# Loading the stacked attention operands in three transfers of 48, 32 and 16 rows

## The chip, the cores and the metric

The kernel runs on one core of one Trainium2 chip. The metric is the device time of one execution in microseconds (us), lower is better. The median of three runs of the kernel before is 3266.39 us (3259.58 to 3267.85).

## The reference

The computation is one block: half a mixture-of-experts feed-forward step, relative-position attention, half a feed-forward step again. The change touches attention alone, whose core is:

```
q, k, v = (w @ Wq.T), (w @ Wk.T), (w @ Wv.T)      # split in 16 heads of 16 values
rp = (r @ Wr.T)                                   # r: 2*Lq-1 sinusoidal positions
AC = einsum('bhid,bhjd->bhij', q + u_bias, k)
BD = einsum('bhid,hjd->bhij', q + v_bias, rp)
BD = _rel_shift(BD)
attn = softmax((AC + BD) * scale)
out = einsum('bhij,bhjd->bhid', attn, v)
```

There are 2 batches of 2048 tokens, so 32 heads in all, each with a score matrix of 2048 x 2048.

## The kernel before

The program has three stages: feed-forward and projections (to about 370 us), attention (to about 3140 us), the last feed-forward.

Each float32 operand of AC and BD is split in three bfloat16 parts that add up to it (`qu_parts`, `qv_parts`, `k_parts`, `pos_parts`, all in DRAM, part number first, then head and value, then position). A product of two float32 numbers becomes six products of parts. So each operand is stacked in SBUF as six blocks of 16 rows, 96 rows (`STACK`), and one matmul over 96 rows sums all six. The query side takes parts `Q_PARTS = (0, 0, 0, 1, 1, 2)`, the key and position side `K_PARTS = (0, 1, 2, 0, 1, 0)`. Rows 0 to 47 thus hold query part 0 three times against key parts 0, 1, 2, rows 48 to 79 query part 1 twice against key parts 0, 1, and rows 80 to 95 query part 2 against key part 0. A row of `qu`, `qv` or `ks` has 2048 values (4 KB), one of `pos` 4096 values (8 KB). All are double buffered. `qu`, `qv` and `ks` are loaded for every head, `pos` for every pair of heads (the same head of the two batches).

Attention goes by tiles of 128 queries, 16 to a head (`NI`), 512 in all. Each engine has a `body(step, k)` for tile k. 192 tiles are written out and run twice in a loop, between 4 tiles ahead and 124 behind. In `body(k)` TensorE (PE) transposes the scores of tile k (line 837), weighs values with it and the tile before (L851), makes position scores for tile k + 15 (L771) and content scores for tile k + 2 (L823). ScalarE (ACT) copies position scores to the buffer `score` (L895, L897) and takes the exponential (L905). VectorE (DVE) adds content and position scores for tile k + 2 (L958) and copies the transposes (L967).

The relative shift is done by DMA. For each group of four tiles GpSimd (POOL) waits for ACT's last copy of the group, and then issues 31 moves `score<-score` (L663) from SBUF to SBUF. Each has an access with two partitions outermost. DVE's first addition of a group waits for them (`moved`); it stands in the body of every fourth tile, with k = 2 modulo 4.

SyncE (SP) issues all loads (`load_head` at L682, `load_pos` at L696, `load_vs` at L701, `store` at L706). Its body names a tile for each block (`QV_BLOCK_AT`, `POS_BLOCK_AT`, `KS_BLOCK_AT`, `VS_AT`), but it has no wait of its own in most tiles. What holds it is `positions_made` before the first block of `qv` (tile 5 of a head) and of `pos` (tile 4 of a pair), `contents_made` before the first block of `ks` (tile 13), the wait for `weighed` before `vs` (tile 9), and the wait for `fin_used` before the store (tile 3). Between these it issues one after another, as fast as it can.

Of the kernel before, what the change touches and what calls it, by code (L numbers as in the profile page):

```python
# [28 lines left out]
Q_PARTS = (0, 0, 0, 1, 1, 2)  # L29
K_PARTS = (0, 1, 2, 0, 1, 0)  # L30
# [3 lines left out]
def build_program(nc, x, wq_t, wk_t, wv_t, wr_t, u_bias, v_bias, w_in, w_out, pos_t, ident, fold, iota, out):  # L34
# [22 lines left out]
    with ctx:  # L57
# [464 lines left out]
        with ExitStack() as c2:  # L522
# [53 lines left out]
            block = c2.enter_context(nc.Block())  # L576
            NLOAD = 16 * len(Q_PARTS)

# [17 lines left out]
            def head_there(step, h):  # L596
                return there(step, h, NT // NI, HEADS)
# [77 lines left out]
            def _(sp):  # L675
                def head(step, h):

                    return h % NB * H + step * (NT // PAIR) + h // NB

                def load_head(dst, src, order, step, h, loaded, blocks):  # L680
                    for i in blocks:
                        sp.dma_start(dst[h % 2][i * DH:(i + 1) * DH, 0:L],  # L682
                                     src[order[i], bass.ds(head(step, h) * DH, DH), :]).then_inc(loaded[h % 2], 16)

                def load_qu(step, h, blocks):
                    load_head(qu, qu_parts, Q_PARTS, step, h, qu_loaded, blocks)

                def load_qv(step, h, blocks):
                    load_head(qv, qv_parts, Q_PARTS, step, h, qv_loaded, blocks)
# [29 lines left out]
                def body(step, k):  # L719
                    h = k // NI + 2  # L720
                    if k % NI in QV_BLOCK_AT and head_there(step, h):
                        if k % NI == QV_BLOCK_AT[0]:
                            positions_made(step, k + POS_AHEAD)
                        load_qv(step, h, [QV_BLOCK_AT.index(k % NI)])
                    pair = k // PAIR + 1
                    if k % PAIR in POS_BLOCK_AT and there(step, pair * PAIR):
                        if k % PAIR == POS_BLOCK_AT[0]:
                            positions_made(step, k + POS_AHEAD)
                        load_pos(step, pair, [POS_BLOCK_AT.index(k % PAIR)])
                    at = (k + NI - KS_FIRST) % NI  # L730
                    h = (k + NI - KS_FIRST) // NI + 1
                    if at in KS_BLOCK_AT and h > 1 and head_there(step, h):
                        if at == 0:
                            contents_made(step, k + AC_AHEAD)
                        load_ks(step, h, [KS_BLOCK_AT.index(at)])
                        load_qu(step, h, [KS_BLOCK_AT.index(at)])
                    h = k // NI + 1
# [7 lines left out]
                for u in range(2):  # L745
                    sp.sem_inc(output_stored[u], 16)
                every = range(len(Q_PARTS))
                load_pos(0, 0, every)
# [368 lines left out]
```

## Time and profile before

| | |
|---|---|
| median of three runs | 3266.39 us |
| profiled execution, its own time | 3262.82 us |
| span of its instructions | 3261.0 us |
| of it attention, first to last transpose | about 2698 us |
| PE, DVE, ACT, POOL busy | 90, 81, 77, 71% |
| data moved by DMA | 657.31 MB, mean 202 GB/s |

The profiled execution stands 3.6 us under the median. "PE busy" includes matmuls that overlap; "idle" in the rows is the engine's time before an instruction, and the name behind an arrow is what ended it. SPq stands for SP's sequencer, and its times are those of issuing a transfer. "Us to landing" runs from issue to the last of a transfer's completions. The share of a DMA queue is the time of its packets, as a share of 16 engines over the span.

### The profile page before, as it was taken

How to read it: one execution, taken by the hardware profiler on the slowest of the kernel's cores; microseconds unless marked ns; L12 is line 12 of the kernel's file. 1: busy time of each engine (PE TensorE's matmuls, PEld its weight loads, DVE VectorE, ACT ScalarE, POOL GpSimd, SP SyncE). 2: the span in 40 equal slices, each digit the busy share in tenths (PEclk: the TensorE clock that was granted, in tenths of full speed). 3: DMA queues.
4: the chain of work that ended last, by engine and by line, in shares of the span. 5: the costliest groups of instructions: out<-in, count | busy, mean ns of one | idle time of the engine just before them, and what ended most of it. 6: DMA issues, size and time to landing. Idle time of an engine off the chain costs nothing. (4 is left out here: it accounts for less than half of the span.)

```text
span 3261.0 us, 110511 instructions
## 1 busy us (share of the span) xinstructions
PE 2923.0 (90%) x40768; PEld 2056.2 (63%) x40768; DVE 2636.0 (81%) x5042; ACT 2501.7 (77%) x3850; POOL 2317.9 (71%) x4135
## 2 busy tenths in 40 slices
PE   4556479999999999998999999999999999999955
PEld 1444146767676767676767666767767676767635
DVE  2555158989898989897989888989989898989976
ACT  2333468989888888887988888888888898889832
POOL 3333487878788878787878888787878787878810
PEclk8777679999999999999999999999999999999977
DMA  6333688888888888887888988888888888888841
GB/s 198 97 110 97 145 205 216 224 217 224 220 221 225 222 217 221 218 221 194 222 219 222 229 216 221 222 218 220 223 221 221 212 225 216 223 224 224 213 128 52
DMA packets 290221, 657.31 MB, mean 202 GB/s; under 512 B 189472, under 2 KB 256928, under 8 KB 272288
## 3 DMA queue, kind: packets, MB, share of 16 engines
q0 software_dynamic: 190960, 526.89, 61.6%
q1 hardware_dynamic: 98736, 123.38, 13.5%
q8 instruction: 335, 5.49, 0.7%
q14 instruction: 190, 1.56, 0.2%
HBM read 77.19 MB, written 46.14 MB: 38 GB/s over the span
## 5 line engine op out<-in xcount | busy, mean ns | idle before, releaser
L663 POOL DMA_DIRECT2D score<-score x3999 | 2186.3, 550 | 560.8 <-ACT score L897 491.4
L895 ACT COPY score<-pos_bank 128x512 f32<-128x512 f32 x2048 | 1105.4, 597 | 330.6 <-PE pos_bank L771 329.0
L905 ACT ACTIVATE score<-score,low 128x1024 f32<-128x1024 f32 x1024 | 1196.9, 1170 | 34.5 <-DVE low L958 30.3
L967 DVE COPY prob_t<-pt_bank 128x512 f32<-128x512 f32 x1792 | 1162.0, 684 | 5.3 <-PE pt_bank L837 2.9
L837 PE MATMUL pt_bank<-ident_sb,score 128*128 128x128 f32 x8192 | 1092.7, 276 | 12.8 <-ACT score L905 6.1
L837 PEld LDWEIGHTS pt_bank<-ident_sb,score 128*128 128x128 f32 x8192 | 958.3, 143 | 225.4 <-issue 52.3
L958 DVE CUSTOM_DVE_ANT_0 score<-ac_bank,score 128x1024 f32<-128x1024 f32 x512 | 627.1, 1225 | 295.5 <-DMA score<-score 153.2
L771 PE MATMUL pos_bank<-pos,qv 96*32 96x512 bf16 (+14 forms) x12160 | 666.5, 318 | 61.9 <-DMA qv<-qv_parts 43.1
L958 DVE CUSTOM_DVE_ANT_0 score<-ac_bank,score,low 128x1024 f32<-128x1024 f32 x512 | 657.2, 1284 | 66.1 <-PE ac_bank L823 58.4
L851 PE MATMUL acc_bank<-prob_t,vs 128*32 128x128 f32 x16384 | 667.0, 280 | 5.6 <-issue 5.5
L823 PE MATMUL ac_bank<-ks,qu 96*128 96x512 bf16 x2048 | 626.5, 388 | 44.8 <-DVE low L958 44.4
L851 PEld LDWEIGHTS acc_bank<-prob_t,vs 128*32 128x32 f32 x16384 | 388.2, 109 | 181.5 <-issue 180.0
L771 PEld LDWEIGHTS pos_bank<-pos,qv 96*32 96x32 bf16 x12160 | 324.9, 98 | 133.2 <-issue 63.0
L823 PEld LDWEIGHTS ac_bank<-ks,qu 96*128 96x128 bf16 x2048 | 116.4, 97 | 363.1 <-DVE low L958 241.7
L509 POOL CAST part<-rest 128x512 bf16<-128x512 f32 x64 | 50.7, 792 | 224.6 <-DVE rest L462 224.6
L913 ACT COPY prob_t<-pt_bank 128x512 f32<-128x512 f32 x256 | 150.0, 586 | 41.8 <-PE pt_bank L837 41.7
L809 PEld LDWEIGHTS pos_bank<-fold_sb,acc_sb 128*128 128x128 f32 x1024 | 135.3, 193 | 21.1 <-issue 2.0
L809 PE MATMUL pos_bank<-fold_sb,acc_sb 128*128 128x32 f32 x1024 | 126.4, 267 | 2.1 <-issue 1.4
L239 PE MATMUL bank_one<-ident_sb,normed_one 128*128 128x128 f32 x128 | 30.2, 426 | 93.4 <-DVE normed_one L148 93.4
L920 ACT COPY acc_sb<-acc_bank 128x512 f32<-128x512 f32 x128 | 75.0, 586 | 30.7 <-PE acc_bank L851 26.0
L462 DVE SCALAR_TENSOR_TENSOR rest<-proj,bias_sb,part 128x512 f32<-128x512 f32 x32 | 36.7, 1212 | 71.7 <-ACT part L443 71.7
L239 PEld LDWEIGHTS bank_one<-ident_sb,normed_one 128*128 128x128 f32 x128 | 25.8, 226 | 98.2 <-DVE normed_one L148 98.2
(95 smaller groups left out, 989.8 us busy)
## 6 DMA issues: line engine op xcount, KB each, us to landing
score<-score POOLq DMA_DIRECT2D x3937, 129.5 KB, 5.4
pos<-pos_parts SPq DMA_DIRECT2D x96, 128.0 KB, 9.7
qv<-qv_parts SPq DMA_DIRECT2D x192, 64.0 KB, 7.2
ks<-k_parts SPq DMA_DIRECT2D x192, 64.0 KB, 7.6
qu<-qu_parts SPq DMA_DIRECT2D x192, 64.0 KB, 7.1
v_heads<-v_sb SPq DMA_DIRECT2D x8, 1024.0 KB, 7.3
vs<-v_heads SPq DMA_DIRECT2D x32, 256.0 KB, 6.9
pos_parts<-part SPq DMA_DIRECT2D x16, 384.0 KB, 3.0
```

The costliest lines, as they stand in the source:

```text
L663: pool.dma_start(shifted(odd, s, groups, 0), shifted(odd, s, groups, QUAD - 1 - s))\
L771: last = pe.matmul(dst[row:row + QUAD, col + lo:col + hi], lhsT=qv[k // NI % 2][:, q0:q0 + QUAD], rhs=pos[u][:, at + lo:at + hi], start=Tr ...
L809: last = pe.matmul(POS[FOLD_AT % 3][:, f * VW:(f + 1) * VW], lhsT=acc_sb[:, f * P:(f + 1) * P], rhs=fold_sb[:, :], start=True, stop=True)
L823: last = pe.matmul(AC[:, c * BANK:(c + 1) * BANK], lhsT=qu[u][:, i * P:(i + 1) * P], rhs=ks[u][:, first:first + BANK], start=True, stop=True)
L837: last = pe.matmul(PT[c % 2][:, t * P:(t + 1) * P], lhsT=score[:, slot(k), c * BANK + t * P:c * BANK + (t + 1) * P], rhs=ident_sb[:, :], i ...
L851: last = pe.matmul(ACC[t * VW:(t + 1) * VW, f * P:(f + 1) * P], lhsT=vs[k // NI % 2][:, 4 * c + t, :], rhs=prob_t[:, c, t * P:(t + 1) * P] ...
L895: act.copy(score[:, at + f, c * BANK:(c + 1) * BANK], ring(m)[:, :]).then_inc(pos_out, 1)
L905: act.activation(cols, cols, ACT.Exp, bias=low[:, slot(k), NH - 1:NH], scale=-1.0)\
L913: act.copy(prob_t[:, c, :], PT[c % 2][:, :]).then_inc(copied_act, 1)
L920: act.copy(acc_sb[:, :], ACC[:, :]).then_inc(acc_out, 1)
L958: dve.tensor_tensor_reduce(cols, AC[:, :], cols, SCALE, low[:, slot(k), h - 1:h] if h else -NEG, ALU.add, ALU.min, low[:, slot(k), h:h + 1 ...
L967: dve.tensor_copy(prob_t[:, c, :], PT[c % 2][:, :]).then_inc(copied, 1)
```

## The change

Each operand is loaded in three transfers (`RUNS = ((0, 3), (3, 2), (5, 1))`: first block and count) of 48, 32 and 16 rows, in place of six of 16 rows. For queries the source is one part, repeated by a zero step in front: its access is 3 (step 0) x 16 x 2048, and 2 x 16 x 2048. For keys and positions it is `k_parts[0:3, 16 rows, :]`, 3 x 16 x 2048 (or x 4096), and 2 x 16. The destination is 48 or 32 partitions. The bytes are the same.

The tiles named for the loads change: `qv` from 5 to 11 of a head to 8, 10, 12; `ks` from 13 to 19 to 13, 15, 17; `qu`, so far beside `ks`, to 19, 21, 23; `pos` from 4 to 11 of a pair to 18, 22, 32; `vs` from 9 to 14.

```diff
-            NLOAD = 16 * len(Q_PARTS)
+            RUNS = ((0, 3), (3, 2), (5, 1))
+            NLOAD = 16 * len(RUNS)
...
-                def load_head(dst, src, order, step, h, loaded, blocks):
+                def rows_of_run(i):
+
+                    return slice(RUNS[i][0] * DH, (RUNS[i][0] + RUNS[i][1]) * DH)
+
+                def load_queries(dst, src, step, h, loaded, blocks):
                     for i in blocks:
-                        sp.dma_start(dst[h % 2][i * DH:(i + 1) * DH, 0:L],
-                                     src[order[i], bass.ds(head(step, h) * DH, DH), :]).then_inc(loaded[h % 2], 16)
+                        part = src[i, bass.ds(head(step, h) * DH, DH), :].rearrange("(o d) n -> o d n", o=1)
+                        sp.dma_start(dst[h % 2][rows_of_run(i), 0:L], part.to_broadcast([RUNS[i][1], DH, L]))\
+                            .then_inc(loaded[h % 2], 16)
...
                 def load_ks(step, h, blocks):
-                    load_head(ks, k_parts, K_PARTS, step, h, ks_loaded, blocks)
+                    for i in blocks:
+                        sp.dma_start(ks[h % 2][rows_of_run(i), :],
+                                     k_parts[0:RUNS[i][1], bass.ds(head(step, h) * DH, DH), :])\
+                            .then_inc(ks_loaded[h % 2], 16)
 
                 def load_pos(step, pair, blocks):
                     for i in blocks:
-                        sp.dma_start(pos[pair % 2][i * DH:(i + 1) * DH, :],
-                                     pos_parts[K_PARTS[i], bass.ds((step * (NT // PAIR) + pair) * DH, DH), :])\
+                        sp.dma_start(pos[pair % 2][rows_of_run(i), :],
+                                     pos_parts[0:RUNS[i][1], bass.ds((step * (NT // PAIR) + pair) * DH, DH), :])\
                             .then_inc(pos_loaded[pair % 2], 16)
...
-                POS_BLOCK_AT = (4, 6, 7, 8, 10, 11)
-                KS_FIRST, KS_BLOCK_AT, QV_BLOCK_AT, VS_AT = 13, (0, 1, 2, 3, 5, 6), (5, 6, 7, 8, 10, 11), 9
+                POS_FIRST, POS_BLOCK_AT = PAIR // 2 + 2, (0, 4, 14)
+                KS_FIRST, KS_BLOCK_AT, QU_BLOCK_AT = 13, (0, 2, 4), (6, 8, 10)
+                QV_BLOCK_AT, VS_AT = (8, 10, 12), 14
...
-                for load in (load_qv, load_ks, load_qu):
+                for load in (load_qv, load_ks):
                     load(0, 1, every)
+                load_qu(0, 1, [i for i in every if QU_BLOCK_AT[i] < FIRST + NI - KS_FIRST])
+                load_pos(0, 1, [i for i in every if POS_BLOCK_AT[i] < PAIR - POS_FIRST])
```

Only SP's instructions change; those of PE, ACT, DVE and POOL stand as they did. Two places on SP, from the pair of heads that begins at tile 32. "ISA" rows are register work and waits; sizes are those of the destination, partitions first.

SP before, in the first half of a pair, from tile 4 on:

```order
L696 ISA [waits pos_full]
L696 DMA pos0<-pos_parts 16x4096
L128 ISA
L682 ISA [waits pos_full]
L682 DMA qv0<-qv_parts 16x2048 x2
L696 ISA
L696 DMA pos0<-pos_parts 16x4096
L682 DMA qv0<-qv_parts 16x2048
```

SP now, from tile 8 on:

```order
L688 ISA [waits pos_full]
L688 DMA qv0<-qv_parts 48x1x2048
L688 ISA
L688 DMA qv0<-qv_parts 32x1x2048
L688 ISA
L688 DMA qv0<-qv_parts 16x2048
```

The blocks of `pos` have gone from here, and `qv` comes three tiles later, in three transfers behind one wait.

SP before, from tile 13 of a pair on, `ks` beside `qu`, six of each, and then the store:

```order
L682 DMA ks0<-k_parts 16x2048 [waits ac_full]
L682 DMA qu0<-qu_parts 16x2048
L682 DMA ks0<-k_parts 16x2048
...
L706 ISA [waits fin_used]
L706 DMA attended<-head_out 128x256
```

SP now, from tile 18 of a pair on:

```order
L705 ISA [waits pos_full]
L705 DMA pos1<-pos_parts 48x1x4096
L688 DMA qu0<-qu_parts 48x1x2048
L128 REGISTER_ALU
L715 ISA [waits fin_used]
L715 DMA attended<-head_out 128x256
L688 DMA qu0<-qu_parts 32x1x2048
L705 DMA pos1<-pos_parts 32x1x4096
L688 DMA qu0<-qu_parts 16x2048
```

Five loads and the store now follow one wait for `pos_full`: the wait for `fin_used` behind it is for work of the same tile.

## Rows read from the trace of the kernel before

**Rows 1.** The page, part 1: busy us, share of the span, instructions.

```profile
PE 2923.0 (90%) x40768; PEld 2056.2 (63%) x40768; DVE 2636.0 (81%) x5042; ACT 2501.7 (77%) x3850; POOL 2317.9 (71%) x4135
```

**Rows 2.** Windows of one head each: heads 13 and 21 (odd), 14 and 20 (even).

```profile
core 0: us, PE busy (x) PEld busy (x) DVE busy (x) ACT busy (x) POOL busy (x), PEclk, DMA share, GB/s
1553.78:1635.24 81.46, 81.46 (x1245) 58.49 (x1244) 74.97 (x129) 73.56 (x114) 67.50 (x124) 1.00 0.83 224
1635.25:1723.17 87.92, 83.93 (x1245) 58.97 (x1244) 74.96 (x129) 73.96 (x114) 67.79 (x125) 0.98 0.84 217
...
2142.70:2230.61 87.91, 84.33 (x1245) 59.45 (x1244) 74.97 (x129) 73.97 (x114) 67.81 (x125) 0.98 0.85 217
2230.62:2312.31 81.69, 81.53 (x1245) 58.51 (x1244) 75.01 (x129) 73.56 (x114) 68.03 (x126) 1.00 0.83 225
```

**Rows 3.** Windows of four tiles each in head 14: tiles 4 to 7, 8 to 11.

```profile
1657.57:1677.94 20.37, 20.37 (x312) 14.69 (x311) 18.76 (x33) 18.38 (x30) 13.88 (x26) 1.00 0.72 187
1677.95:1702.81 24.86, 22.14 (x312) 15.28 (x311) 18.72 (x33) 18.57 (x30) 20.78 (x39) 0.93 1.04 260
```

**Rows 4.** Waits of DVE from 500 to 3100 us: us in total, times, longest.

```profile
DVE score L958 <- PE ac_bank L823: 184.2, 337, 4.2
DVE score L958 <- DMA score<-score: 86.9, 37, 6.6
```

**Rows 5.** Timeline in head 14, DVE, then PE: start, duration, instruction, idle time before.

```profile
1691.79 1.23 DVE L958 CUSTOM_DVE_ANT_0 score<-ac_bank,score 128x1024 f32<-128x1024 f32 x1 [4.22 <-DMA score<-score]
...
1691.84 0.87 PE L837 MATMUL pt_bank<-ident_sb,score 128*128 128x128 f32 x5 [2.72 <-issue]
1692.64 1.08 PE L851 MATMUL acc_bank<-prob_t,vs 128*32 128x128 f32 x16
```

**Rows 6.** Timeline of SP's issues in head 14.

```profile
1667.26 2.46 SPq L682 DMA_DIRECT2D qv<-qv_parts  x2
1669.91 1.80 SPq L696 DMA_DIRECT2D pos<-pos_parts  x1
...
1677.05 1.85 SPq L696 DMA_DIRECT2D pos<-pos_parts  x1
1684.79 0.35 SPq L701 DMA_DIRECT2D vs<-v_heads  x1
```

**Rows 7.** Timeline of POOL's issues in head 14: one group's moves, the next begin.

```profile
1667.02 14.76 POOL L663 DMA_DIRECT2D score<-score  x27 [1.10 <-issue]
1684.09 16.40 POOL L663 DMA_DIRECT2D score<-score  x30 [2.31 <-ACT score L897]
```

**Rows 8.** DMA queues from 500 to 3100 us: packets, MB, share of 16 engines.

```profile
q0 software_dynamic: 183083, 506.17, 74.2%
q1 hardware_dynamic: 28633, 58.21, 8.6%
```

**Rows 9.** DMA issues of the whole run: transfers, KB each, median us to landing.

```profile
score<-score POOLq DMA_DIRECT2D x3937, 129.5 KB, 5.4
pos<-pos_parts SPq DMA_DIRECT2D x96, 128.0 KB, 9.7
qv<-qv_parts SPq DMA_DIRECT2D x192, 64.0 KB, 7.2
...
vs<-v_heads SPq DMA_DIRECT2D x32, 256.0 KB, 6.9
...
qu_parts<-part SPq DMA_DIRECT2D x16, 384.0 KB, 2.9
...
score<-score POOLq DMA_DIRECT2D x62, 64.8 KB, 2.8
```

**Rows 10.** Timeline at the start of attention: SP's first issues, PE's first matmuls.

```profile
372.68 2.68 SPq L696 DMA_DIRECT2D pos<-pos_parts  x6
375.41 2.73 SPq L682 DMA_DIRECT2D qv<-qv_parts  x6
...
383.88 1.94 PE L771 MATMUL pos_bank<-pos,qv 96*32 96x32 bf16 x20 [43.08 <-DMA qv<-qv_parts]
```

More of the change, by code:

```diff
@@ L678, in head @@
                     return h % NB * H + step * (NT // PAIR) + h // NB
-                def load_head(dst, src, order, step, h, loaded, blocks):
+                def rows_of_run(i):
+                    return slice(RUNS[i][0] * DH, (RUNS[i][0] + RUNS[i][1]) * DH)
+                def load_queries(dst, src, step, h, loaded, blocks):
                     for i in blocks:
-                        sp.dma_start(dst[h % 2][i * DH:(i + 1) * DH, 0:L],
-                                     src[order[i], bass.ds(head(step, h) * DH, DH), :]).then_inc(loaded[h % 2], 16)
+                        part = src[i, bass.ds(head(step, h) * DH, DH), :].rearrange("(o d) n -> o d n", o=1)
+                        sp.dma_start(dst[h % 2][rows_of_run(i), 0:L], part.to_broadcast([RUNS[i][1], DH, L]))\
+                            .then_inc(loaded[h % 2], 16)
                 def load_qu(step, h, blocks):
-                    load_head(qu, qu_parts, Q_PARTS, step, h, qu_loaded, blocks)
+                    load_queries(qu, qu_parts, step, h, qu_loaded, blocks)
                 def load_qv(step, h, blocks):
-                    load_head(qv, qv_parts, Q_PARTS, step, h, qv_loaded, blocks)
+                    load_queries(qv, qv_parts, step, h, qv_loaded, blocks)
                 def load_ks(step, h, blocks):
-                    load_head(ks, k_parts, K_PARTS, step, h, ks_loaded, blocks)
+                    for i in blocks:
+                        sp.dma_start(ks[h % 2][rows_of_run(i), :],
+                                     k_parts[0:RUNS[i][1], bass.ds(head(step, h) * DH, DH), :])\
+                            .then_inc(ks_loaded[h % 2], 16)
                 def load_pos(step, pair, blocks):
                     for i in blocks:
-                        sp.dma_start(pos[pair % 2][i * DH:(i + 1) * DH, :],
-                                     pos_parts[K_PARTS[i], bass.ds((step * (NT // PAIR) + pair) * DH, DH), :])\
+                        sp.dma_start(pos[pair % 2][rows_of_run(i), :],
+                                     pos_parts[0:RUNS[i][1], bass.ds((step * (NT // PAIR) + pair) * DH, DH), :])\
                             .then_inc(pos_loaded[pair % 2], 16)
@@ L724, in body @@
                         load_qv(step, h, [QV_BLOCK_AT.index(k % NI)])
-                    pair = k // PAIR + 1
-                    if k % PAIR in POS_BLOCK_AT and there(step, pair * PAIR):
-                        if k % PAIR == POS_BLOCK_AT[0]:
+                    at = (k + PAIR - POS_FIRST) % PAIR
+                    pair = (k + PAIR - POS_FIRST) // PAIR + 1
+                    if at in POS_BLOCK_AT and there(step, pair * PAIR):
+                        if at == 0:
                             positions_made(step, k + POS_AHEAD)
-                        load_pos(step, pair, [POS_BLOCK_AT.index(k % PAIR)])
+                        load_pos(step, pair, [POS_BLOCK_AT.index(at)])
                     at = (k + NI - KS_FIRST) % NI
@@ L735, in body @@
                         load_ks(step, h, [KS_BLOCK_AT.index(at)])
-                        load_qu(step, h, [KS_BLOCK_AT.index(at)])
+                    if at in QU_BLOCK_AT and (h > 1 or k >= FIRST) and head_there(step, h):
+                        load_qu(step, h, [QU_BLOCK_AT.index(at)])
                     h = k // NI + 1
@@ L746, in _ @@
                     sp.sem_inc(output_stored[u], 16)
-                every = range(len(Q_PARTS))
+                every = range(len(RUNS))
                 load_pos(0, 0, every)
```

## The prediction

> **What bounds the kernel now.** I read the page's busy shares first, then windows of one head each, and then the waits and the timeline where a head is slow. PE is busy 90% of the span, more than any other engine [rows 1], and in a quiet head it is busy all the time: head 13 takes 81.46 us with 81.46 us of PE, and head 21 81.69 us with 81.53 [rows 2]. That is the floor, 32 heads of it. It is not reached in even heads: heads 14 and 20 take 87.9 us for the same work [rows 2]. The four tiles 4 to 7 of head 14 still take 20.37 us, at a DMA share of 0.72; tiles 8 to 11 take 24.86 us, at a share of 1.04 (it can pass 1 by what is counted at a window's edge), and there PE is busy 22.14 us only, at a granted clock of 0.93 [rows 3]. The reader should see that PE does the same 312 matmuls and that the DMA engines are full. The timeline names the link: DVE waited 4.22 us for the moves `score<-score`, PE then stood for 2.72 us, and the 16 matmuls of L851 behind the stop took 1.08 us [rows 5]. Over the steady stretch DVE lost 86.9 us in 37 such waits; its larger sum for `ac_bank` is PE's own pace [rows 4].
>
> How thin the cover is follows from two rows. POOL's issues for that group ended at 1667.02 + 14.76 = 1681.78 us [rows 7]. DVE wanted the data at 1691.79 - 4.22 = 1687.57 us [rows 5]. So moves may land 5.8 us after the last issue; their median is 5.4 [rows 9]. Whatever adds more than half a microsecond to the landing of the last moves is paid in full. (A group's cover is about 1.1 us longer where POOL has not had the extra stop of 1.10 us that stands in rows 7.)
>
> **What the change removes.** The loads of `pos` leave the stretch in which `qv` and `vs` are loaded, and `qv` comes three tiles later. SP issued `qv` and `pos` in turn behind one wait, 1.2 us each or more, from 1667.26 to about 1679 us, inside the time in which the group's moves are issued and land [rows 6, 7]. With `pos` gone the share there falls back to that of an odd head. Odd heads show the result: 6.2 us less than the even ones in rows 2. Other even heads lose less, and the 86.9 us of rows 4 hold all such waits. I take 4.4 us for each of 16 even heads, 70 us. The bounds are 50 and 87 us. SP's issues fall from six to three for each operand; SP is waited for by nobody in the steady stretch, so I cost that at nothing.
>
> **What it adds: the same bytes on fewer DMA engines.** The question on which the sum turns is how many of the 16 DMA engines a transfer of 48 rows uses. The trace shows no such load, but it shows what an access with a small outermost count does. A move has two partitions outermost. With one stretch in each it carries 64.8 KB and lands after 2.8 us, with two stretches 129.5 KB after 5.4 us, while 384 KB with 128 partitions outermost land after 2.9 us [rows 9]. A transfer that was spread over 16 engines would not take 2.6 us longer for 65 KB. So two rows run on about two engines. The new sources have 3 or 2 outermost (with step 0 for queries), whatever the destination has. I take it that the 48-row transfers run on three engines and the 32-row ones on two, and that these are always the same, since no rotation shows for SP; that last point is an assumption.
>
> The Trainium skill (DMA: Bandwidth & Descriptors, "Why a DMA increments its semaphore by 16 and not by 1") says that the count of engines is the largest number up to 16 that divides both accesses' slowest dimension, and that a load from SP uses the lowest-numbered ones; by it the counts are 3 and 2, and the sum is the one below. No run here has shown it for loads from SP.
>
> The price. Queue q1 moved 58.21 MB in 8.6% of 16 engines' 2600 us, 3578 us of engine time, and q0 506.17 MB in 74.2%, 30867 us [rows 8]: 61 us a MB for both. A 48-row load of 196.6 KB gives each of three engines 65.5 KB, 4.0 us; a 32-row load gives each of two the same, 4.0 us; 16 rows on 16 engines give 4 KB, 0.25 us. `pos` has double rows, 8.0, 8.0 and 0.5 us. The two engines that are in both counts get, for each head, 3 x 8.25 us for `qv`, `ks` and `qu` and half of 16.5 for `pos`, 33 us. Before, each engine had 3 x 6 x 0.25 + 3 x 0.5 = 6 us. That is 27 us more for each head. The engines stand idle 16% of a head (shares of 0.83 to 0.85 [rows 2]), 13 us. So 14 us a head find no room: 450 us over 32 heads is the upper bound. The lower is 0: the 61 us a MB were measured with all 16 engines in each other's way, and 14 engines now lose some of their load, so the two may run faster and swallow all.
>
> Between these I go by the clumps, since that is what rows 5 show to be paid. In each pair of heads there are five places where one or two 4.0 us shares fall on the two engines while moves are in flight (`qv` at tiles 8 and 24, `ks` at 13 and 29, `qu` at 31, which nothing holds back), and one at tile 18 with 8 + 4 + 4 + 8 = 24 us behind a single wait. A move issued to these engines waits at least for the share ahead of it. With half a microsecond of cover, and some 2 us that the engines are idle between two groups' moves, I put 1 us on each of the five and 7 us on the 24 us clump, since moves and loads take turns and two groups share it. That is 12 us a pair, 190 us for 16 pairs. It is nearer to the lower bound than to the upper, because rows 3 show what an overfull stretch costs: tiles 8 to 11 of head 14 ran at a share of 1.04 and lost 4.5 us, not more.
>
> The first loads are on the path too. PE's first matmul waits for `pos` and `qv`, from the first issue at 372.68 us to 383.88 us [rows 10]. Now the two engines have 16.5 + 8.25 = 25 us of work before `qv` is whole, at the rate above, and at least half of it on an idle chip. The start comes 3 to 15 us later; I take 10. The loads of the next head and `pos` pair are queued right behind and meet the first moves: 3 us.
>
> The sum, against the profiled execution's own 3262.8 us: -70 + 190 + 13 = +133, 3396 us. The median of the runs stands 3.6 us higher, within their spread; I say **3395 us**.
>
> **Rivals.**
>
> *Sixteen engines after all (chance 0.20).* If 48 rows are spread by the destination, three rows to an engine, the bytes of each engine stay as they were and the collision goes: -70 us. Against that stands the clump of tile 18: 384 + 192 + 128 + 128 + 256 + 64 KB, 1.18 MB, 4.5 us on each engine, of which some 2 us were there before (`ks` and `qu`). 2.5 us more, less the 1.1 us of looser cover, is 1.4 us for each of 16 pairs, 22 us, and 10 us for `qv` closer to a landing. 3225 us: **faster**. For it: the destination's outermost count is a multiple of 16. Against it: the moves of rows 9. It decides at one point: whether source or destination sets the spread.
>
> *Few engines, but the moves slip through (0.12).* If an engine takes one packet of a load and one of a move in turn, 4 KB (0.25 us) ahead of each 2 us of a move delay the moves by an eighth only, and the loads bear the wait, which have over ten tiles to land. Then 50 us take the place of the 190: 3255 us, from no change to slightly faster. Against it: `vs` has 8 rows of 2 KB for each engine and `qv` one of 4 KB, and both land after about 7 us [rows 9]; eight turns behind moves would be longer by 14 us.
>
> The Trainium skill (DMA: Bandwidth & Descriptors, "Queues, rings and completion order") has each engine drain some 9 to 17 descriptors of one ring before it turns to another. By it a share of 16 rows passes in one or two turns, and the forecast holds; by turns of one it would be this rival. Rows 9 agree with the first in `vs`.
>
> *Two engines full (0.08).* If the 14 us a head are all paid: 3263 - 70 + 450 + 13, about 3655 us.
>
> **How the numbers follow.** The forecast has 0.60, with a range of its own from 3290 to 3540 us: its stalls can be 80 or 340 us. Of a difference under 0.3%, some 10 us, a measurement can't tell much from no change. The first rival is faster in 0.17 of its 0.20, the second in 0.05 with 0.04 within 0.3%, the forecast's low end gives 0.02 faster and 0.03 the same: faster 0.24, same 0.09, slower 0.67. The range for 8 in 10 leaves out the lower half of the first rival and the last one: 3220 to 3560 us.
>
> **What the profile will show.** If I am right, the 48-row and 32-row loads take 10 us and more to land while a 16-row one stays near 7; DVE's wait for the moves rises from 86.9 us to over 200; odd heads are slow as well as even ones, with the worst four tiles from 20 to 27 of a pair; the granted clock falls below 0.99; and the mean DMA share falls, since the span grows and the bytes don't. PE's start comes at 387 us or later. If the loads land after 7 or 8 us at every size and tiles 8 to 11 of even heads take 20.4 us, it was the first rival. If large loads land late and the wait for the moves is small, it was the second. What would break the sum without touching the mechanism is the clump of tile 18, its largest and least certain term.

## The result and the profile after

The changed kernel takes 3558.58 us, the median of 4 runs (3550.05 to 3564.23), beside 3265.6 us for the kernel before, the median of 4 (3259.58 to 3267.85). The ratio is 1.0883, interval 1.0859 to 1.0906: slower by 293 us where 129 was forecast. The profiled execution took 3550.05 us, 287.2 more than the profiled one before.

First part 1 of the page of after, then its DMA queue of SP's transfers (packets, MB, share of 16 engines), then windows of one head each: head 14 (even), head 15 (odd).

```profile
PE 2975.7 (84%) x40768; PEld 2083.4 (59%) x40768; DVE 2633.7 (74%) x5042; ACT 2504.0 (71%) x3850; POOL 2309.9 (65%) x4135
...
q1 hardware_dynamic: 90336, 123.35, 12.0%
```

```profile
core 0: us, PE busy (x) PEld busy (x) DVE busy (x) ACT busy (x) POOL busy (x), PEclk, DMA share, GB/s
1776.07:1871.83 95.76, 84.56 (x1245) 59.86 (x1244) 74.96 (x129) 73.69 (x114) 67.55 (x125) 0.93 0.74 196
1871.84:1960.98 89.14, 84.40 (x1245) 59.52 (x1244) 74.92 (x129) 73.69 (x114) 67.35 (x124) 0.96 0.78 209
```

No engine's busy time rose by more than 3 us but PE's, whose 2923.0 us [rows 1] became 2975.7 for the same instructions. Its granted clock in these heads is 0.93 and 0.96, where even and odd ones had 0.98 and 1.00 [rows 2]: a part of the time is spent at 1.2 GHz rather than 2.4, behind stops such as the one shown below (0.80 in its four tiles). Both kinds of head are slow now. The DMA share, 0.83 to 0.85 before, fell to 0.74 and 0.78, with the same bytes: the DMA engines taken together have more room than before, and data comes later all the same.

Next, the waits of DVE in after from 500 to 3400 us (total, times, longest).

```profile
DVE score L972 <- DMA score<-score: 358.4, 61, 14.5
DVE score L972 <- PE ac_bank L837: 180.3, 284, 2.7
```

The wait for the moves rose by 271 us, from 86.9 in 37 waits to 358.4 in 61 [rows 4]; the wait for PE stayed. Most of the loss sits in one place. Here are two windows of four tiles in after, tiles 0 to 3 of an even head (16) and of an odd one (17), and then the timeline around tile 2 of head 16: SP's issues, POOL's, DVE and PE.

```profile
1960.99:1994.72 33.73, 23.35 (x312) 16.03 (x311) 18.72 (x33) 18.56 (x30) 20.88 (x39) 0.80 0.78 208
2055.84:2077.31 21.47, 21.05 (x312) 14.41 (x311) 18.72 (x33) 18.57 (x30) 19.41 (x37) 1.00 0.87 234
```

```profile
1948.34 0.75 SPq L699 DMA_DIRECT2D ks<-k_parts  x1
1953.17 0.36 SPq L710 DMA_DIRECT2D vs<-v_heads  x1
1953.62 0.67 SPq L699 DMA_DIRECT2D ks<-k_parts  x1
1954.40 0.72 SPq L705 DMA_DIRECT2D pos<-pos_parts  x1
1955.22 1.51 SPq L699 DMA_DIRECT2D ks<-k_parts  x1
1956.82 0.75 SPq L688 DMA_DIRECT2D qu<-qu_parts  x1
```

```profile
1950.80 14.18 POOL L664 DMA_DIRECT2D score<-score  x26 [0.18 <-issue]
1967.13 16.89 POOL L664 DMA_DIRECT2D score<-score  x31 [2.16 <-ACT score L911]
```

```profile
1983.03 1.23 DVE L972 CUSTOM_DVE_ANT_0 score<-ac_bank,score 128x1024 f32<-128x1024 f32 x1 [12.00 <-DMA score<-score]
...
1984.32 1.03 PE L837 MATMUL ac_bank<-ks,qu 96*128 96x512 bf16 x2 [10.18 <-DVE low L972]
```

POOL's last issue of the group ended at 1950.80 + 14.18 = 1964.98 us. DVE could go on at 1983.03, so the last move landed 18 us after its issue, where rows 9 have a median of 5.4. In the ten microseconds ahead of 1957.6, while PE was in tiles 29 to 31 of the pair of heads before, SP had put out six loads, those of its steps 29 to 35: three parts of `ks`, `vs`, the last part of `pos`, and the 48-row part of `qu`. PE stood still for 10.18 us.

For the accounts below I use one measure, worked out from the trace for all kernels: the 511 tile steps of attention, each from one tile's transposes to the next's, minus the time of the same tile of four in a quiet head (20.36 us for all four), summed by the tile's place in a pair of heads (0 to 31, 16 pairs). I call it the excess.

| place in the pair | excess before | after | forecast term |
|---|---|---|---|
| tiles 8 to 11 | 71 | 0.5 | -70, collision gone |
| tile 18 | 5 | 19 | `ks` at 13: 16 |
| tiles 22 and 26 | 0 | 132 | clump of tile 18: 109 |
| tile 2 | 6 | 183 | `ks` at 29 and `qu` at 31: 31 |
| all of attention | 95 | 350 | |

The forecast's 1 and 7 us a pair stand here over 16 pairs at tile 18 and over 15.5 at the other two places, since the last pair has no next one to load for.

Attention grew by the same 255 us, from 2697.8 to 2952.4. The rest is the start: DVE's first wait for the moves ends 32.5 us later than before. With these 32.5 the sum is 287 us, all that the profiled executions differ by. First the line of before, then those of after, SP's first issue among them.

```profile
432.56 1.22 DVE L958 CUSTOM_DVE_ANT_0 score<-ac_bank,score 128x1024 f32<-128x1024 f32 x1 [59.85 <-DMA score<-score]
```

```profile
373.46 2.08 SPq L705 DMA_DIRECT2D pos<-pos_parts  x3
...
394.44 1.94 PE L785 MATMUL pos_bank<-pos,qv 96*32 96x32 bf16 x20 [52.86 <-DMA qv<-qv_parts]
...
465.11 1.23 DVE L972 CUSTOM_DVE_ANT_0 score<-ac_bank,score 128x1024 f32<-128x1024 f32 x1 [91.63 <-DMA score<-score]
```

### The profile page after: what moved, and what is told of

The parts are those of the page before. It is cut to its first block and busy times, and to the rows that moved or that the text cites. A ratio compares the mean times of both kernels' runs of the same rounds, so it can differ in the third digit from the quotient of the medians.

```text
span 3548.3 us, 109904 instructions
## 1 busy us (share of the span) xinstructions
PE 2975.7 (84%) x40768; PEld 2083.4 (59%) x40768; DVE 2633.7 (74%) x5042; ACT 2504.0 (71%) x3850; POOL 2309.9 (65%) x4135
## 3 DMA queue, kind: packets, MB, share of 16 engines
q1 hardware_dynamic: 90336, 123.35, 12.0%
## 5 line engine op out<-in xcount | busy, mean ns | idle before, releaser
L851 PE MATMUL pt_bank<-ident_sb,score 128*128 128x128 f32 x8192 | 1115.7, 280 | 7.3 <-issue 4.6
L851 PEld LDWEIGHTS pt_bank<-ident_sb,score 128*128 128x128 f32 x8192 | 977.4, 145 | 234.1 <-DVE prob_t L981 59.3
L837 PE MATMUL ac_bank<-ks,qu 96*128 96x512 bf16 x2048 | 641.7, 396 | 294.3 <-DVE low L972 291.6
L785 PE MATMUL pos_bank<-pos,qv 96*32 96x512 bf16 (+15 forms) x12160 | 670.3, 321 | 56.8 <-DMA qv<-qv_parts 52.9
L865 PE MATMUL acc_bank<-prob_t,vs 128*32 128x128 f32 x16384 | 676.7, 284 | 2.2 <-issue 1.9
L972 DVE DVE_READ_ACCUMULATOR2_ANT low<- 128x1 f32 x1024 | 85.4, 83 | 0.0
```

The costliest lines, as they stand in the source:

```text
L785: last = pe.matmul(dst[row:row + QUAD, col + lo:col + hi], lhsT=qv[k // NI % 2][:, q0:q0 + QUAD], rhs=pos[u][:, at + lo:at + hi], start=Tr ...
L837: last = pe.matmul(AC[:, c * BANK:(c + 1) * BANK], lhsT=qu[u][:, i * P:(i + 1) * P], rhs=ks[u][:, first:first + BANK], start=True, stop=True)
L851: last = pe.matmul(PT[c % 2][:, t * P:(t + 1) * P], lhsT=score[:, slot(k), c * BANK + t * P:c * BANK + (t + 1) * P], rhs=ident_sb[:, :], i ...
L865: last = pe.matmul(ACC[t * VW:(t + 1) * VW, f * P:(f + 1) * P], lhsT=vs[k // NI % 2][:, 4 * c + t, :], rhs=prob_t[:, c, t * P:(t + 1) * P] ...
L972: dve.tensor_tensor_reduce(cols, AC[:, :], cols, SCALE, low[:, slot(k), h - 1:h] if h else -NEG, ALU.add, ALU.min, low[:, slot(k), h:h + 1 ...
```

## The experiments

The theory: a load whose source has 3 or 2 outermost occupies three or two DMA engines for a long time, and moves on these engines come late. The rivals: the bytes are spread over 16 and it is the tiles at which they are now loaded that cost; or larger transfers as such are in the way.

**The same tiles, sixteen engines.** Two kernels keep every tile of after. In the first each run of 48, 32 or 16 rows is issued as three, two or one transfers of 16 rows.

```diff
-                        part = src[i, bass.ds(head(step, h) * DH, DH), :].rearrange("(o d) n -> o d n", o=1)
-                        sp.dma_start(dst[h % 2][rows_of_run(i), 0:L], part.to_broadcast([RUNS[i][1], DH, L]))\
-                            .then_inc(loaded[h % 2], 16)
+                        for r in of_run(i):
+                            sp.dma_start(dst[h % 2][r * DH:(r + 1) * DH, 0:L],
+                                         src[Q_PARTS[r], bass.ds(head(step, h) * DH, DH), :]).then_inc(loaded[h % 2], 16)
```

> The changed kernel with the same tiles and waits, but each transfer of 48 or 32 rows issued as three or two of 16 rows. Theory of few engines: the 16-row loads use all 16 engines, so the stalls go. The excess of 350 us over a quiet head's pace falls under 60 us: about 3215 us (3190 to 3270), ratio to before 0.98 to 1.00, and DVE's waits for the moves fall from 358 us (500 to 3400 us) to under 70. Rival, the tiles: what costs is that five loads and a store now stand behind one wait. Then this kernel stays over 3450 us, since it issues the same bytes behind the same waits.

The second keeps the three large transfers and turns round the two outer dimensions of the source, so that the 16 values come first and the repeats second (the stacked rows then lie value by part in both operands of the product, which leaves the sum over them the same).

```diff
-                        part = src[i, bass.ds(head(step, h) * DH, DH), :].rearrange("(o d) n -> o d n", o=1)
-                        sp.dma_start(dst[h % 2][rows_of_run(i), 0:L], part.to_broadcast([RUNS[i][1], DH, L]))\
+                        part = src[i, bass.ds(head(step, h) * DH, DH), :].rearrange("(d o) n -> d o n", o=1)
+                        sp.dma_start(dst[h % 2][rows_of_run(i), 0:L], part.to_broadcast([DH, RUNS[i][1], L]))\
...
-                                     k_parts[0:RUNS[i][1], bass.ds(head(step, h) * DH, DH), :])\
+                                     k_parts[0:RUNS[i][1], bass.ds(head(step, h) * DH, DH), :].rearrange("s d n -> d s n"))\
```

> The changed kernel with its three transfers, but with the 16 values outermost in the source and the repeat (or the part) behind them: the 48 rows lie as value by part instead of part by value, on both sides of the product, so the sum is the same. Both accesses then have outermost counts of 16 and 48, or 16 and 32. Theory of few engines set by the smaller outermost count: 48 packets go to 16 engines, 3225 us (3190 to 3270), and queue q1 counts 98736 packets again less the completions of 336 fewer transfers (5376). Rival, the size of a transfer: 192 KB and 384 KB transfers stop the moves whatever engines they run on; then it stays over 3450 us while e1 is fast. Rival, the tiles: both stay over 3450.

Measured: 3291.99 us with 16-row transfers (ratio 1.0071, interval 1.0041 to 1.0100) and 3337.22 us with the values first (1.0214, 1.0166 to 1.0263). So of the 293 us the dimension that comes first in the source makes 221, the larger transfers as such, at these tiles, 45, and the new tiles 26. Both kernels are slower than the 3190 to 3270 us that I expected: with sixteen engines 129 and 170 us of excess are left, so the tiles cost too. DVE's waits for the moves, from 500 to 3400 us, fell from 358.4 to these, first with 16 rows, then with the values first:

```profile
DVE score L974 <- DMA score<-score: 101.4, 31, 5.6
```

```profile
DVE score L973 <- DMA score<-score: 125.7, 31, 8.0
```

SP's queue on the pages of the 16-row kernel, of the values-first one and, from its list of DMA issues, a large load with its landing time:

```profile
q1 hardware_dynamic: 98736, 123.38, 13.6%
```

```profile
q1 hardware_dynamic: 93360, 123.36, 13.5%
...
pos<-pos_parts SPq DMA_DIRECT2D x16, 256.0 KB, 13.9
```

The packets count the engines. Loads of the four operands before are 672 transfers, in after 112 sets of three. If each engine that a transfer uses writes one packet of its own at the end, 16 engines for each of 336 transfers give 98736 - (672 - 336) x 16 = 93360 packets, and that is what the values-first kernel has. With 3, 2 and 16 engines for a set it is 98736 - 672 x 16 + 112 x 21 = 90336, which is what after has. The Trainium skill (DMA: Bandwidth & Descriptors, "Why a DMA increments its semaphore by 16 and not by 1") gives these counts, as the largest number up to 16 that divides the outermost counts of both sides; the packets agree to the last one. By size it is the packets of 4 bytes alone that differ: the trace has 14128 of them with 16 rows, 8752 with the values first and 5728 in after, and as many as before of every other size. Nor are the packets slower with few engines: the times of all packets of q1 add up to 6799 us in after and to 7221 with the values first.

**The loads two tiles apart or where they were.** The 48, 32 and 16 rows in the kernel before, at its own tiles.

```diff
-                POS_BLOCK_AT = (4, 6, 7, 8, 10, 11)
-                KS_FIRST, KS_BLOCK_AT, QV_BLOCK_AT, VS_AT = 13, (0, 1, 2, 3, 5, 6), (5, 6, 7, 8, 10, 11), 9
+                POS_BLOCK_AT = (4, 7, 10)
+                KS_FIRST, KS_BLOCK_AT, QV_BLOCK_AT, VS_AT = 13, (0, 2, 5), (5, 7, 10), 9
```

> The kernel before with the three transfers of 48, 32 and 16 rows (part outermost) at tiles of its own schedule: qv 5, 7, 10; pos 4, 7, 10; ks and qu 13, 15, 18; vs 9. Theory of few engines: engines 0 and 1 get the same 33 us a head as in the changed kernel, but in two heaps: qv with pos in the first half of a pair (24 us), ks with qu in each head (16 us). Slower than the changed kernel or like it: 3500 to 3750 us. Rival, the tiles: it is like the kernel before, 3240 to 3290 us.

Measured: 3906.25 us (1.1959, 1.1885 to 1.2033), beyond what was expected. The waits of DVE for the moves, from 500 to 3400 us:

```profile
DVE score L967 <- DMA score<-score: 651.9, 52, 21.9
```

The excess lies at tiles 2, 10 and 18 of the pair, 196, 312 and 185 us, each behind a place where loads on few engines follow each other. With few engines the new tiles thus gain 348 us over those of before; with 16-row transfers they lose 26. What the loads cost hangs on both, and the number of engines is the larger part.

**What fills tile 2.** The costliest place wasn't the one that I had priced highest. Two theories: `qu` following `ks`, `vs` and `pos` makes the clump; or the engines still carry work from tiles 18 to 26. First `qu` two steps later, out of the stretch.

```diff
-                KS_FIRST, KS_BLOCK_AT, QU_BLOCK_AT = 13, (0, 2, 4), (6, 8, 10)
+                KS_FIRST, KS_BLOCK_AT, QU_BLOCK_AT = 13, (0, 2, 4), (8, 10, 12)
```

> The changed kernel with qu at 21, 23, 25 in place of 19, 21, 23, so that the first qu transfer of an even head stands behind the wait of the store at tile 3 and not in one row with ks, vs and pos at tiles 29 to 31. Theory: the load is paid only above what the two engines have free within one group's moves. With 4 us less on them before tile 34 the stall of tile 2 of a pair (183 us of excess in all) falls to what tile 18 has (19 us, the same loads but for pos), and the group of tile 6 takes the 8 us of qu with under 2 us a pair: 3400 to 3440 us. Rival: the excess of tile 2 comes from ks and vs themselves, or the work is conserved and only moves to tile 6: then it stays within 40 us of 3558.

Measured: 3525.70 us (1.0794, 1.0709 to 1.0878). Tile 2 went from 183 to 127 us, not to 19, and tile 26 rose from 38 to 99, since `qu` of the other head now falls there. The time stayed within 40 us of 3558, as the rival had it. Then few engines for `ks` and `qu` alone, and for `qv` and `pos` alone, the others with the values first.

```diff
+                        if spread:
+                            part = part.rearrange("(d o) n -> d o n", o=1).to_broadcast([DH, RUNS[i][1], L])
+                        else:
+                            part = part.rearrange("(o d) n -> o d n", o=1).to_broadcast([RUNS[i][1], DH, L])
```

> The changed kernel, with qv and pos on 16 engines (values outermost, as in e2) and ks and qu left on three and two. In front of tile 34 stand the same loads on engines 0 and 1 as in the changed kernel (13 us from ks, vs and qu), but the 32 us of pos, qu and qv that fall on them from tile 18 to 25 are cut to 10. Theory of a backlog that is carried from group to group: the excess of tile 2, 183 us in the changed kernel, falls to 60 to 110; total 3360 to 3440 us. Rival, each heap for itself: the excess of tile 2 stays at 170 to 190 us, since its own loads are unchanged; total over 3440.

> The other half: ks and qu on 16 engines, qv and pos on three and two. Engines 0 and 1 get 33 us a pair from them. In front of tile 34 nothing but 16-engine loads stands, as in e1 and e2, where tile 2 had 38 us of excess. Theory of the carried backlog: pos and qv of tiles 18 to 25 are worked off by tile 29 when no ks and qu follow on the same engines, so tile 2 has about 38 us, and tiles 22 and 26 60 to 130 together; total 3350 to 3430 us. If the sum of e5's and e6's loss over e2 is well under the changed kernel's 221 us over e2, the loss is that of an overfull engine and not of single transfers; if it is the same, each transfer pays for itself.

Measured: 3462.81 us (1.0603, 1.0569 to 1.0637) and 3448.89 us (1.0561, 1.0529 to 1.0593). DVE's waits for the moves, from 500 to 3400 us, in the one and the other:

```profile
DVE score L977 <- DMA score<-score: 266.4, 44, 13.9
```

```profile
DVE score L976 <- DMA score<-score: 243.0, 33, 17.1
```

With `qv` and `pos` on sixteen engines tiles 22 and 26 are almost clear (48 us at tile 22, as in the values-first kernel with its 56), and tile 2 keeps 176 of its 183 us. So nothing is carried over from tiles 18 to 26, and tile 2 is due to `ks` and `qu` right ahead of it. The other kernel has 189 us at tile 22 and 39 at tile 2. Over the values-first kernel the two halves cost 126 and 112 us, 237 together, and after has 221. The totals nearly add, but the places don't: at tile 2 the sum of the two is right, while at tiles 22 and 26 after has 132 us, less than the 189 that `qv` and `pos` alone make there. Why few engines for `ks` and `qu` as well make these two places cheaper isn't shown.

**What of tile 2 is whose.** The last 16 rows of `pos` at SP's step 26 rather than 32, out of the stretch (these are on sixteen engines), and both moves together.

```diff
-                POS_FIRST, POS_BLOCK_AT = PAIR // 2 + 2, (0, 4, 14)
+                POS_FIRST, POS_BLOCK_AT = PAIR // 2 + 2, (0, 4, 8)
```

> The changed kernel with one thing moved: the 16-row block of pos goes from tile 32 of a pair to tile 26. In e5 tile 2 kept 176 us of excess although the backlog from tiles 18 to 25 was gone, so that theory fell: the heap of tiles 29 to 31 pays for itself. Tile 18, with the same ks and vs in front, has 19 us. What tile 2 has more is the 16-row pos block (0.5 us on each engine) and the 48-row qu (4 us on three). Theory: the block of pos is the larger part, because it stands on all 16 engines and on 0 and 1 behind two shares of ks; then the excess of tile 2 falls from 183 to 80 us or less and the time to about 3460. Rival: it counts by its engine time, 0.5 us in 13.75; then tile 2 keeps over 160 us and the time stays at 3540 to 3570.

> e4's and e8's moves together in the changed kernel: qu at 21, 23, 25 and the last block of pos at 26, so that tiles 29 to 31 issue ks and vs only, the loads that tile 13 to 15 issue. Each move alone took 56 and 44 us from the 183 us of excess at tile 2. If the parts add, 83 us stay. If the cost of a heap grows faster than its size, tile 2 falls to what tile 18 has with the same loads, 20 us (under 45). The time tells little of it, since tiles 22 and 26 take over what is moved there: 3440 to 3530 us.

Measured: 3512.38 us (1.0764, 1.0710 to 1.0819) and 3493.78 us (1.0709, 1.0625 to 1.0793). Tile 2 has 139 us and 88 us. For the first I had expected 80 or less, or else over 160; it is neither. `qu` is worth 56, the last part of `pos` 44, and the two together 95, so they add. What is left, 88 us, is `ks` and `vs` alone. At tile 18 the odd heads' `ks` and `vs` stand just so before the moves, and there it is 13.5 us. That difference of 75 us has no cause that these runs show. It is not the time of issue: with both moved, the first three loads go out 16.5, 11.6 and 11.2 us before the end of the group's last issue at both places and the 16-row `ks` 10.4 us before it at tile 2 and 9.0 at tile 18, yet the last move lands some 11 us after that issue at tile 2 and 7.6 at tile 18.

**Can it be had for nothing?** If full use of sixteen engines is the point, the loads should cost nothing at tiles where the moves have 1.1 us more cover. From the 16-row kernel, `pos` goes to SP's steps 24, 40 and 41 of the pair (8 and 9 of the next one) and `qu` to three steps in a row:

```diff
-                POS_FIRST, POS_BLOCK_AT = PAIR // 2 + 2, (0, 4, 14)
-                KS_FIRST, KS_BLOCK_AT, QU_BLOCK_AT = 13, (0, 2, 4), (6, 8, 10)
+                POS_FIRST, POS_BLOCK_AT = PAIR // 2 + 8, (0, 16, 17)
+                KS_FIRST, KS_BLOCK_AT, QU_BLOCK_AT = 13, (0, 2, 4), (7, 8, 9)
```

> A version meant to beat both: 16-row transfers as in e1, with qu behind the store at tile 3 of a head (group with the longer cover), and pos in two halves, three rows behind qv at tile 24 of a pair and three behind qv at tile 8 of the next. e1 showed no stall at tiles 10, 14, 18, 26 and 30 of a pair, and its two heaps (pos with qu at 18; ks, vs, pos and qu at 29 to 31) are gone here. Theory: the excess falls from 129 us in e1 to 30 to 50 us: 3195 to 3225 us. Rival, the bytes have to be paid wherever they stand: about 3265, like the kernel before.

Measured: 3236.09 us (0.9908, 0.9886 to 0.9929). The moves are on time (DVE waits 27.7 us for them in all, from 500 to 3100 us), yet the kernel is slower than the 3195 to 3225 us that I expected, and an excess of 73 us is left. Some 50 of them are at tiles 12 and 13 and 28 to 30, where PE stands with nothing shown that it waits for. This is its largest row of that kind among the waits, same stretch:

```profile
PE pos_bank L787 <- issue: 17.7, 17, 3.0
```

So the 16-row loads were grouped at four places for `pos` and one or two for each other operand. The note below names the change of `pos` alone, but `qv`, `ks` and `qu` are bunched as well.

```diff
-            RUNS = ((0, 3), (3, 2), (5, 1))
+            RUNS = tuple((i, 1) for i in range(6))
...
-                POS_FIRST, POS_BLOCK_AT = PAIR // 2 + 8, (0, 16, 17)
-                KS_FIRST, KS_BLOCK_AT, QU_BLOCK_AT = 13, (0, 2, 4), (7, 8, 9)
-                QV_BLOCK_AT, VS_AT = (8, 10, 12), 14
+                POS_FIRST, POS_BLOCK_AT = PAIR // 2 + 2, (0, 6, 6, 18, 22, 22)
+                KS_FIRST, KS_BLOCK_AT, QU_BLOCK_AT = 13, (0, 0, 0, 2, 2, 2), (7,) * 6
+                QV_BLOCK_AT, VS_AT = (8,) * 6, 14
```

> e7 with the three rows of pos at tile 24 and the three at tile 40 taken apart: one block at 18, two at 24, one at 36, two at 40. In e7 only the group of tile 30 landed its moves later than its cover (9.7 us on average, others under 7.8), and tiles 28 to 30 held 39 of 73 us of excess. Theory: with two blocks there it lands within cover, and the excess falls to 40 to 60 us: 3210 to 3225 us. Rival: the excess of tiles 28 and 29 comes from late instruction fetches of PE and not from the moves; they follow the DMA load as a whole and stay: 3230 to 3240 us, like e7.

And the values-first kernel, with its three large transfers, at the tiles of the first of these two kernels (the first diff of tiles above):

> e7's tiles with e2's transfers: 48, 32 and 16 rows on 16 engines. e2 lost 45 us against e1 at the same tiles, so large transfers cost something even when spread: three packets for each engine stand together in front of moves. Theory: the loss comes only where the group's cover is used up, and e7's tiles leave room, so it is under half: 3240 to 3260 us. Rival: fewer transfers are an advantage once the tiles are calm: under 3230 us. Third: the loss stays as it was: 3275 us or more.

Measured: 3199.92 us (0.9808, 0.9777 to 0.9839) and 3198.94 us (0.9811, 0.9771 to 0.9852). Both are faster than the kernel before by 1.9%. The first is faster than the 3210 to 3225 us expected; which of its changes did it, these runs don't separate. For the second I expected 3240 to 3260 us, with large transfers still behind small ones, and that was wrong. Its like is the 16-row kernel with the same steps, 3236.09 us: there the large transfers are 37 us faster, where at the tiles of after they were 45 us slower. The excess fell from 73 us to 23, all of it at the tiles where PE had stood without a shown cause. The rival, that fewer transfers are an advantage once the tiles are calm, is what came. The values-first kernel at the calm tiles, part 1 of its page and its queue, two heads in a row, DVE's wait from 500 to 3100 us:

```profile
PE 2894.6 (91%) x40768; PEld 2050.0 (64%) x40768; DVE 2635.3 (83%) x5042; ACT 2494.5 (78%) x3850; POOL 2310.1 (72%) x4135
...
q1 hardware_dynamic: 93360, 123.36, 13.9%
```

```profile
core 0: us, PE busy (x) PEld busy (x) DVE busy (x) ACT busy (x) POOL busy (x), PEclk, DMA share, GB/s
1603.58:1686.99 83.41, 81.98 (x1245) 58.62 (x1244) 75.16 (x129) 73.53 (x114) 67.36 (x125) 1.00 0.84 222
1687.00:1768.46 81.46, 81.46 (x1245) 58.54 (x1244) 74.98 (x129) 73.47 (x114) 67.38 (x124) 1.00 0.87 230
```

```profile
DVE score L973 <- DMA score<-score: 12.9, 13, 2.3
```

Head 14 takes 83.4 us where it took 87.9, head 15 stands at the floor of rows 2, and the granted clock is 1.00 in both.

**The disputed cost by itself.** The last kernel has the same tiles, the same number of transfers and the same bytes as this one. It differs in the source's order alone: parts first, as in after.

```diff
-                        part = src[i, bass.ds(head(step, h) * DH, DH), :].rearrange("(d o) n -> d o n", o=1)
-                        sp.dma_start(dst[h % 2][rows_of_run(i), 0:L], part.to_broadcast([DH, RUNS[i][1], L]))\
+                        part = src[i, bass.ds(head(step, h) * DH, DH), :].rearrange("(o d) n -> o d n", o=1)
+                        sp.dma_start(dst[h % 2][rows_of_run(i), 0:L], part.to_broadcast([RUNS[i][1], DH, L]))\
```

> e10 with nothing changed but the order of the source: parts outermost, as in the changed kernel, so that the 48-row and 32-row transfers run on three and two engines. e10 has 23 us of excess and 3199 us. By engine time the two lowest engines still get 66 us a pair in place of 12. Theory of few engines: most of the loss stays whatever the tiles: 3400 us or more. Rival: e10's gain over the changed kernel is the tiles' own; then under 3300 us.

Measured: 3722.87 us (1.1412, 1.1312 to 1.1512), 524 us more than with the values first. Its queue on the page, and DVE's wait for the moves from 500 to 3600 us:

```profile
q1 hardware_dynamic: 90336, 123.35, 11.7%
```

```profile
DVE score L972 <- DMA score<-score: 514.1, 59, 20.1
```

The excess is at tiles 6, 14, 22 and 30 of the pair (73, 178, 49 and 220 us). These are the places at which sixteen-engine loads cost nothing. The cause is settled by this pair of kernels: the same bytes, issued at the same steps, differ by 524 us through the dimension that stands first.

## Why the prediction was off

- **What bounds the kernel.** Right. The link from late moves to DVE to PE carries the loss: DVE's wait for the moves grew by 271 us in the steady stretch, and attention as a whole by 255.
- **The collision, -70.** Right: tiles 8 to 11 of even heads fell from 71 us of excess to 0.5.
- **Three and two engines.** Right; the packets show 3, 2 and 16.
- **The signs in the profile.** The wait rose over 200, odd heads are slow too, the clock fell below 0.99, the mean DMA share fell, PE's start came after 387 us: all as foretold. The worst four tiles were to be 20 to 27 of a pair. They are 0 to 3, with 33.7 us in the even head shown against 21.5 in the odd one. The list of DMA issues gives no landing time for loads on three and two engines, but the semaphore updates in the trace do: `ks`, `qv` and `qu` are complete 12.3, 12.6 and 11.2 us after the issue of their last transfer, the one of 16 rows (medians of the steady stretch), where before it was 7.4, 8.4 and 6.5. So loads land late, but the 16-row one doesn't stay near 7 us as foretold: it stands behind the others on the two engines.
- **PE's first matmul, 10 us.** Right: 10.6 us later. The two engines that are in all transfers of `pos` and `qv` had 0.41 MB each to bring in the 21 us from the first issue at 373.46 us, so at most 52 us a MB on a chip without moves, where I had 61 beside them.
- **The clump of tile 18, 7 us a pair.** Nearly right: 132 us at tiles 22 and 26 of 15.5 pairs are 8.5 us a pair. The `ks` at tile 13, put at 1 us, cost 0.9.
- **The step that failed** is "there are five places where one or two 4.0 us shares fall on the two engines", 1 us for each, as it was put for `ks` at 29 and `qu` at 31. I counted these two as singles, 2 us a pair, 31 in all. They are issued 8 us apart, with `vs`, the other parts of `ks` and the last part of `pos` between them, all ahead of the end of the same group of moves. They are a clump of shares like that of tile 18, and it cost 177 us over before, 11 us a pair. That is 146 of the 154 us by which the profiled execution passed the sum; the other misses nearly cancel (clump of tile 18 +23, start +20, `qv` -31). The rule that priced tile 18 right, shares summed ahead of one group of moves, wasn't applied here. Even so it would have given 3 or 4 us a pair, at most 7, and not 11, for three 4.0 us shares against six; `vs` and the last `pos` were not in it at all, and the run that moved the last `pos` shows 44 us for these rows on sixteen engines. So the price of a clump was too low as well, and the 88 us that `ks` and `vs` alone leave there say that its size alone doesn't set it. Of the other singles `qv` at tile 8 cost nothing; `qv` at tile 24 can't be told from the clump ahead of tile 26, but with `qv` and `pos` alone on few engines tile 26 has no excess.
- **The next head's loads against the first moves, 3 us.** Wrong: 32.5 us in all at the start, less the 10.6 of PE, are 22 us. It looks like the same omission, though no run takes the start apart: `qv`, `ks`, `qu` and now `pos` are queued right behind, and these are the shares of a whole clump of loads, not of a single one. The values-first kernel has its first wait for the moves end at 431.66 us, as before.
- **The bound.** The stalls of after stay under 450 us, but that was no bound. The 48, 32 and 16 rows at the tiles of the kernel before cost 641 us over it, the order of dimensions alone 524 at the calm tiles. It was worked out from time that the engines stand idle over a head; but a group's moves are late by what is ahead of them at their time, whatever idle time follows.
- **The rivals.** Sixteen engines after all would have given 3292 or 3337 us and not 3225: the new tiles are worse for the moves than I had read, 26 us slower than those of before with 16-row transfers, since `pos`, `ks` and `qu` come close in front of tile 2 and tile 22 even so (39 and 45 us). Moves that slip through didn't come: 221 to 524 us say that they don't. Two engines full, at 3655 us, is not what came either: the loss stands at few places, and with `qv` and `pos` on sixteen engines tile 2 keeps its own. No row shows how busy a single engine is, so how near to full the two are stays open.

**What stays open.** The 88 us that `ks` and `vs` alone leave at tile 2, beside 13.5 for the same loads at tile 18. Moves use about two engines each, by rows 9, and it may be that which group's last moves fall on the loaded engines repeats with the pair of heads. The count fits: 31 moves on two engines each are 62 for a group and 496, or 31 times 16, for the eight groups of a pair, so if moves take the engines in turn, a place in the pair meets the same engines every time, and the two places, half a pair apart, meet engines eight apart. No row shows the engine of a move and no run changed their number, so this is a guess. Nor do the runs separate whether loads and moves take turns packet by packet or in longer stretches.

## What to carry to other kernels

Before joining small loads into large ones, look at the outermost count on both sides of each transfer, and put a dimension that 16 divides there, even if the repeats or parts must go inside and the rows be stacked in another order. Sum the loads' shares by DMA engine and by the group of latency-bound transfers that they precede, also across the end of a head or a loop pass: the DMA share of a window didn't show the trouble, since it fell while the time rose. Whether joining pays at all depends on the place: with sixteen engines it cost 45 us at one set of tiles and gained 37 at the other. The right order of dimensions and a few loads moved by some steps turned 9% slower into 2% faster, with the same number of transfers.

## What the runs showed that I had not expected

- The number of engines that a load uses cost 524 us at one set of steps and 221 at another, for 123.35 MB of queue q1, while all kernels with sixteen engines, whatever their tiles and the size of their transfers, lie between 3199 and 3337 us.
- The price is paid in the granted clock too: PE's busy time for the same 40768 instructions goes from 2894.6 us with a wait of 12.9 us for the moves, over 2923.0 with 86.9, to 2975.7 with 358.4, at mean granted clocks of 0.950, 0.945 and 0.910.
- At crowded tiles large transfers on sixteen engines are worse than small ones by 45 us (3337 against 3292), and at calm tiles, with the same steps, better by 37 (3198.94 against 3236.09). The Trainium skill (DMA: Bandwidth & Descriptors, "Rules for kernel authors") says to coalesce many small transfers; the runs agree at the second set of tiles and not at the first.
- With the moves on time a new floor shows: PE's stops without a shown cause at a few tiles. All excess is 73 us in the first 16-row kernel at the calm tiles and under 30 in the two fastest. In the traces of the two 16-row kernels at calm tiles PE has 27 stops of over 0.8 us from 500 to 3060 us, and 23 of them end 1.3 to 1.8 us after a packet of the instruction queue (q8) has ended, though these packets come 8 us apart (median); that points to the fetch of instructions beside loads; no run tested it.
